# Layer-1 attention: the values' transpose moved to a slot's head, the output product moved to the next batch

## The reference

```python
qkv = x @ qkv_w.T + qkv_b                       # 16 heads of 8
scores = einsum('bhid,bhjd->bhij', q, k) / sqrt(8)
scores = scores + _alibi_bias(16, 256, 0.5)     # -|i - j| * slope[h]
attn = softmax(scores)
out = einsum('bhij,bhjd->bhid', attn, v)
x = x + (out @ out_w.T + out_b)
```

## Time and profile before

| what | value |
|---|---|
| median of 3 runs | 1610.66 us (1606.85 to 1613.25) |
| the profiled execution's own time | 1614.27 us |
| its span | 1612.5 us |
| mean granted TensorE clock over the span | 0.962 of full |
| TensorE busy over the span | 1464.5 us (91%) |
| VectorE busy over the span | 1071.1 us (66%) |
| ScalarE busy over the span | 1007.6 us (62%) |
| layer-1 attention's slots | about 950 to 1340 us of the span |

### The profile page before, as it was taken

How to read it: one execution, slowest core, us unless ns; L and a number is a source line. 1 busy time by engine, 2 the same in 40 slices (tenths; PEclk the granted TensorE clock), 3 DMA queues, 4 the chain that set the end, 5 groups by cost and what they waited for, 6 DMA issues and landing times. The chain is left out here.

```text
span 1612.5 us, 39525 instructions
## 1 busy us (share of the span) xinstructions
PE 1464.5 (91%) x11702; PEld 1106.8 (69%) x11703; DVE 1071.1 (66%) x3467; ACT 1007.6 (62%) x2671; POOL 503.1 (31%) x861
## 2 busy tenths in 40 slices
PE   7999999999999877889999878888888886999998
PEld 5777777777777644578888745555555554777697
DVE  6776777767777466656666537778777763775565
ACT  6887887878878446246666546666666663554454
POOL 4332333323333236033333131322223103552133
PEclk9999999999999987889999979999999997998999
DMA  6000000000000031011111110000000000000000
GB/s 212 2 0 0 0 0 0 0 0 0 0 0 1 25 152 33 27 30 42 46 42 42 33 52 9 13 13 7 13 13 11 8 2 0 2 1 1 1 27 26
DMA packets 34077, 35.77 MB, mean 22 GB/s; under 512 B 5472, under 2 KB 29664, under 8 KB 33120
## 3 DMA queue, kind: packets, MB, share of 16 engines
q1 hardware_dynamic: 29664, 26.08, 5.0%
q0 software_dynamic: 4352, 8.92, 2.2%
HBM read 26.07 MB, written 8.91 MB: 22 GB/s over the span
## 5 line engine op out<-in xcount | busy, mean ns | idle before, releaser
L671 POOL TENSOR_SCALAR a_prob<-a_prob,a_inv 128x128 f32<-128x128 f32 (+1 forms) x256 | 126.4, 504 | 336.5 <-DVE a_inv L547 336.5
L474 ACT ACTIVATE a_prob<-a_psS,a_low 128x128 f32<-128x128 f32 (+1 forms) x512 | 208.8, 427 | 0.9 <-DVE a_low L537 0.9
L537 DVE CUSTOM_DVE_ANT_0 a_psS<-a_psS,a_bias 128x128 f32<-128x128 f32 (+1 forms) x512 | 167.5, 388 | 42.8 <-PE a_psS L322 38.6
L1831 ACT ACTIVATE a_probT<-a_psZ 128x512 f32<-128x512 f32 x256 | 139.1, 595 | 89.3 <-PE a_psZ L1617 70.7
L1914 DVE TENSOR_REDUCE a_low<-a_psS 128x4 f32<-128x1024 f32 x128 | 156.2, 1220 | 52.9 <-remote 34.6
L465 ACT COPY a_probT<-a_psT 128x384 f32<-128x384 f32 x256 | 122.6, 479 | 77.7 <-PE a_psT L368 69.1
L368 PE MATMUL a_psT<-ident,a_prob 128*128 128x128 f32 x768 | 132.8, 282 | 3.7 <-ACT a_probT L465 1.8
L1357 POOL DMA_INDIRECT d_rows<-rows_dram,source x72 | 68.2, 947 | 187.2 <-PE e_psX L1440 134.7
L322 PE MATMUL a_psS<-a_qk 64*128 64x128 f32 (+1 forms) x1024 | 120.0, 353 | 3.2 <-issue 1.4
L368 PEld LDWEIGHTS a_psT<-ident,a_prob 128*128 128x128 f32 x768 | 84.7, 140 | 45.4 <-issue 34.3
L358 PE MATMUL a_psO<-a_probT,a_v 128*64 128x256 f32 (+1 forms) x1024 | 111.5, 339 | 0.0
(11 more groups left out here) (376 smaller groups left out, 4159.2 us busy)
## 6 DMA issues: line engine op xcount, KB each, us to landing
sorted_out<-e_y SPq DMA_DIRECT2D x72, 64.0 KB, 1.5
in_lo<-in_gate_up SPq DMA_DIRECT2D x4, 1024.0 KB, 7.9
x<-in_x SPq DMA_DIRECT2D x8, 256.0 KB, 6.8
down<-in_down SPq DMA_DIRECT2D x1, 2048.0 KB, 16.5
rows_dram<-rows SPq DMA_DIRECT2D x8, 256.0 KB, 2.2
out<-x SPq DMA_DIRECT2D x8, 256.0 KB, 2.3
d_rows<-rows_dram,source POOLq DMA_INDIRECT x72
cw<-in_count_wide SPq DMA_DIRECT2D x1, 1024.0 KB, 4.7
```

The costliest lines, as they stand in the source:

```text
L474: nc.scalar.activation(prob[:, 2 * (p % 4) + k, lo:hi], psS[:, u, lo:hi], ACT.Exp, bias=low[:, u, i:i + 1], scale=-1.0, accum_out=total[:, ...
L537: nc.vector.tensor_tensor_reduce(psS[:, u, lo:hi], psS[:, u, lo:hi], bias0[:, 2 * p + k, lo:hi], 1.0, LEAST, ALU.add, ALU.min, low[:, u, i ...
L671: nc.gpsimd.tensor_scalar(w, w, inv[:, 2 * (q % 2) + 1, i:i + 1], 1.0, ALU.mult, ALU.mult).then_inc(norm_done[1], 1)
L1831: nc.scalar.activation(probT[:, (p + half + 1) % 2, 2 * half + c, :, :].rearrange("p j s -> p (j s)"), psZ[:, c, :], ACT.Exp, scale=-1.0). ...
```

## The change

1. `turn_values` moves from between the first and the second scores to the head of the next slot, ahead of `turn_lows`. It then needs no wait for `shift` of the same slot, but for that of the slot before. `oT` gets two buffers, as the unit's result now lies one slot longer. `divide` handles the unit that is four slots old (p - 4) instead of three, and `turn_lows` no longer waits for `o_norm`.
2. The transpose of `o_rows` (`turn_rows`) and the copy to `o_cols` move from slot 2 to slot 3, ahead of `values`.
3. The product with `wo1` (`output`) moves from the end of slot 2 to the head of slot 0 of the next batch.
4. `choice_kept` and `out_statistics` move from slot 3, where they stand on either side of `lows(b, 3, 1)`, to slot 0 of the next batch, where both stand between `divide` and `lows(b, 0, 1)`.
5. `ln.apply`, `ln.turn` and `ln.keep` move from slot 0 to slot 1. On VectorE `ln.apply` stands there between `divide` and `statistics`.

```diff
--- before.py
+++ after.py
@@ -1546,7 +1546,7 @@
         low = ph.sb("low", [P, 2, BT, P])
         probT = ph.sb("probT", [P, 2, 4, BT, S])
         v_aug = ph.sb("v_aug", [P, BT, H, VW])
-        oT = ph.sb("oT", [P, S])
+        oT = ph.sb("oT", [P, 2, S])
         inv = ph.sb("inv", [P, BT, 4])
         o_rows = ph.sb("o_rows", [P, BT, D])
         o_cols = ph.sb("o_cols", [P, S])
@@ -1684,23 +1684,39 @@
                 pe.wait_ge(low_done, n * 2)
                 if not (isinstance(b, int) and b == 0 and p == 1):
                     pe.wait_ge(qm4_done, n - 1)
-                if not (isinstance(b, int) and b == 0):
-                    pe.wait_ge(o_norm, n - 3)
                 for i in range(BT):
                     mm = pe.transpose(psT[:, i * P:(i + 1) * P], low[:, (p + 1) % 2, i, :], g.ident[:])
                 mm.then_inc(lowt_done, 1)
 
-            def turn_values(b, p, lagging):
+            def turn_values(b, p, new):
 
                 n = b * 4 + p
-                pe.wait_ge(o_kept, n - 2)
-                if lagging:
-                    pe.wait_ge(qm4_done, n)
+                pe.wait_ge(o_kept, n - 3)
+                if new or p < 2:
+                    pe.wait_ge(qm4_done, n - 1)
+                if not (isinstance(b, int) and b == 1 and p == 0):
+                    pe.wait_ge(o_norm, n - 4)
+                for i in range(BT):
+                    mm = pe.transpose(psT[:, S + i * P:S + (i + 1) * P], oT[:, p % 2, i * P:(i + 1) * P], g.ident[:])
+                mm.then_inc(ot_done, 1)
+
+            def turn_rows(b, prep):
+
+                pe.wait_ge(o_norm, b * 4)
+                if prep:
+                    pe.wait_ge(cur_ready, b + 2)
                 else:
-                    pe.wait_ge(o_norm, n - 3)
+                    ln.wait_kept(pe, b - 1)
                 for i in range(BT):
-                    mm = pe.transpose(psT[:, S + i * P:S + (i + 1) * P], oT[:, i * P:(i + 1) * P], g.ident[:])
-                mm.then_inc(ot_done, 1)
+                    mm = pe.transpose(psM[:, i * P:(i + 1) * P], o_rows[:, i, :], g.ident[:])
+                mm.then_inc(oc_done, 1)
+
+            def output(count):
+
+                pe.wait_ge(oc_kept, count)
+                for i in range(BT):
+                    mm = pe.matmul(psM[:, i * P:(i + 1) * P], o_cols[:, i * P:(i + 1) * P], g.wo1[:], start=True, stop=True)
+                mm.then_inc(y_done, 1)
 
             def context_keys():
 
@@ -1740,12 +1756,14 @@
                 for p in range(4):
                     old, older = has_unit(p, 4), has_unit(0, 8)
                     n = b * 4 + p
+                    if p == 0 and older:
+                        output(b - 1)
+                    if old:
+                        turn_values(b, p, new)
                     if has_unit(p, 1):
                         turn_lows(b, p)
                     if new or has_unit(p, 2):
                         first_scores(b, p, new, has_unit(p, 2))
-                    if has_unit(p, 3):
-                        turn_values(b, p, has_unit(p, 1))
                     if new and p < 3:
                         if p == 2:
                             pe.wait_ge(v_kept, b + 1)
@@ -1762,16 +1780,8 @@
                         ln_in.turn(pe, b + 1, psM)
                     if new or has_unit(p, 1):
                         second_scores(b, p, new, has_unit(p, 1))
-                    if p == 2 and old:
-
-                        pe.wait_ge(o_norm, b * 4)
-                        if prep:
-                            pe.wait_ge(cur_ready, b + 2)
-                        else:
-                            ln.wait_kept(pe, b - 1)
-                        for i in range(BT):
-                            mm = pe.transpose(psM[:, i * P:(i + 1) * P], o_rows[:, i, :], g.ident[:])
-                        mm.then_inc(oc_done, 1)
+                    if p == 3 and old:
+                        turn_rows(b, prep)
                     if has_unit(p, 2):
                         values(b, p)
                     if new and p == 1:
@@ -1782,15 +1792,11 @@
                     if prep and p == 2:
                         pe.wait_ge(qk4_kept, n + 2)
                         project(b + 1)
-                    if p == 2 and old:
-                        pe.wait_ge(oc_kept, b)
-                        for i in range(BT):
-                            mm = pe.matmul(psM[:, i * P:(i + 1) * P], o_cols[:, i * P:(i + 1) * P], g.wo1[:], start=True, stop=True)
-                        mm.then_inc(y_done, 1)
-                    if p == 0 and older:
+                    if p == 1 and older:
                         pe.wait_ge(y_used, b - 1)
                         ln.turn(pe, b - 2, psM)
                     if p == 3 and not new:
+                        output(b)
                         pe.wait_ge(y_used, b)
                         ln.turn(pe, b - 1, psM)
 
@@ -1863,17 +1869,17 @@
                         keep_in(b + 1)
                     if has_unit(p, 1):
                         exps(b, p, 0)
-                    if p == 2 and old:
+                    if p == 3 and old:
                         act.wait_ge(oc_done, b)
                         nc.scalar.copy(o_cols[:], psM[:, 0:S]).then_inc(oc_kept, 1)
                     if has_unit(p, 2):
                         act.wait_ge(pv_done, n - 1)
-                        if not (isinstance(b, int) and b == 0 and p == 2):
-                            act.wait_ge(ot_done, n - 2)
-                        nc.scalar.copy(oT[:], psO[:, 0:S]).then_inc(o_kept, 1)
+                        if old:
+                            act.wait_ge(ot_done, n - 3)
+                        nc.scalar.copy(oT[:, p % 2, :], psO[:, 0:S]).then_inc(o_kept, 1)
                     if prep and p == 2:
                         keep_qk(b + 1)
-                    if p == 0 and older:
+                    if p == 1 and older:
                         ln.keep(act, b - 2, psM[:, 0:S], act_seen)
                     if p == 3 and not new:
                         ln.keep(act, b - 1, psM[:, 0:S], act_seen)
@@ -1923,14 +1929,13 @@
                 v.tensor_tensor(qm4[:, (p + 1) % 2, :], psT[:, 0:S], qk4[:, G, 0, :].bitcast(F32), ALU.add).then_inc(qm4_done, 1)
 
             def divide(b, p):
-                m = b * 4 + p - 3
-                G = (p + 1) % 4
+                m, G = b * 4 + p - 4, p
                 dve.wait_ge(ot_done, m + 1)
                 rows = psT[:, S:2 * S].rearrange("p (i h c) -> p i h c", i=BT, c=VW)
                 v.reciprocal(inv[:], rows[:, :, :, DH1]).then_inc(inv_done, 1)
                 dve.wait_ge(inv_done, m + 1)
-                if p == 3 and not (isinstance(b, int) and b == 0):
-                    dve.wait_ge(oc_done, b)
+                if p == 0 and not (isinstance(b, int) and b == 1):
+                    dve.wait_ge(oc_done, b - 1)
                 for i in range(BT):
                     x = v.tensor_tensor(o_rows[:, i, 4 * G * DH1:4 * (G + 1) * DH1].rearrange("p (h c) -> p h c", h=4),
                                         rows[:, i, :, 0:DH1], inv[:, i, :].unsqueeze(2).to_broadcast([P, 4, DH1]), ALU.mult)
@@ -1983,14 +1988,15 @@
                         split_lo(b + 1)
                     if new:
                         lows(b, p, 0)
-                    if has_unit(p, 3):
+                    if old:
                         divide(b, p)
                     if p == 0 and older:
+                        choice_kept(b - 1)
+                        out_statistics(b - 1)
+                    if p == 1 and older:
                         ln.apply(dve, b - 2)
                     if prep and p == 1:
                         statistics(b + 1)
-                    if p == 3 and old:
-                        choice_kept(b)
                     if new:
                         lows(b, p, 1)
                     if prep and p == 0:
@@ -1998,9 +2004,9 @@
                         add_choice(b + 1, 1)
                     if prep and p == 1:
                         ln_in.apply(dve, b + 1)
-                    if p == 3 and old:
+                    if p == 3 and not new:
+                        choice_kept(b)
                         out_statistics(b)
-                    if p == 3 and not new:
                         ln.apply(dve, b - 1)
 
             rounds_of_four(dve, first, slots)
```

## The result

The changed kernel took 1638.94 us (median of 4 runs, 1637.33 to 1642.62), the kernel before beside it 1611.95: a ratio of 1.0172, 95% interval 1.0142 to 1.0203. It is 1.7% slower. Its profiled execution took 1639.7 us with a span of 1637.9, against 1614.27 and 1612.5.

A forecast was written before the change was run, and what follows sets the result against it. The prediction took the ring of VectorE reductions through psS, not TensorE's busy share, as the bound. Terms -0.25 + 1.0 + 0.7 + 0.62 gave +2.07 us a batch, +28 overall: 1638 against the median, range 1618 to 1648.

The forecast's parts named there:

- a ring of reductions: Eight VectorE reductions per batch: scores await the reduction ahead to free psS, the next reduction awaits scores; legs total 23.56 us.
- Slot 2: Two legs between reduction starts, 8.03 us together; forecast gain 0.25 us a batch from ScalarE losing o_cols, bounds 0 and 1.35.
- The head: Slot 3's second leg, 2.80 us, into slot 0's head: TensorE's longer queue ahead of turn_lows adds 1.0 us, bounds 0.91 to 1.29.
- Slot 0's first leg: Leg of 2.33 us: VectorE loses ln.apply, gains choice_kept and out_statistics; forecast +0.7 us, bounds 0.6 and 0.8.
- Slot 1's first leg: Leg of 2.37 us, full on VectorE: ln.apply comes on top; forecast +0.62 us, bounds 0.55 and 0.64.
- The batch: One batch of the loop, slot 2 to slot 2: forecast +2.07 us, 25.6 instead of 23.56.
- The drain: The draining tail at the kernel's end: called the same serial chain, with no added time forecast.
- Rival 1: Slot 2: the hold goes with TensorE's removed wait, gaining 1.35 us a batch; 14 us less than forecast, 1624; chance 0.22.
- the hold: Slot 2, first leg: TensorE's completions reach other engines late while gathers are under way, 1.10 us a batch; forecast to stay.
- rival 2: Every slot: faster, as TensorE bounds them, its two waits vanish and nothing on VectorE shows; 11 us less, 1600; chance 0.11.
- rival 3: No change: the hold goes and slot 0's extra VectorE work is covered; 0.3 us a batch, 1614; chance 0.11.
- rival 4: More than forecast: the head costs 1.29 us, slot 0 0.8, and slot 2's ScalarE chain gains nothing; 1647; chance 0.04.

The follow-up runs named there:

- e3: Changed kernel with the edits of e1 and e2, and the output product between the first and second scores of slot 0; 1589.9 us, ratio 0.998.
- b_before: The kernel before, unchanged, traced again in the second group, on a chip without the hold; 1587.93 us in one run.
- a_after: The changed kernel once more, without the hold, against the kernel before; 1618.05 us against 1593.07, ratio 1.0148.
- e8: e3 with layer-norm transposes between slot 1's scores, and slot 2's query/key projection and scaling put first; without the hold 1578.3 us, ratio 0.990.
- e9: Changed kernel with one line moved: output product between the first and second scores of slot 0 instead of at its head; ratio 1.0081.
- e1: Changed kernel with part 1 undone: values' transpose back between the scores, one oT, o_rows' transpose beside it in slot 3; 1613.92 us, ratio 1.0133.
- e2: Changed kernel with layer-norm statistics moved to slot 2, application to slot 3's end, its transpose and copy to the next batch's slot 1; ratio 1.0063.
- b2_before: The kernel before, unchanged, traced again in the third group, on a chip with the hold; 1623.6 us in one run.
- e10: The kernel before without the gathers of batches 2 to 15, on a chip with the hold; 1592.62 us against 1616.95, ratio 0.9856.
- e6: The kernel before with the gathers issued in slot 0 of the next batch, one batch further ahead, on a chip without the hold; ratio 1.0003.
- e11: The same kernel as e8, run again on a chip with the hold; 1628.9 us against 1616.95 for the kernel before, ratio 1.0075.
- e4: The kernel before without the gathers of batches 2 to 15, on a chip without the hold; ratio 0.9976.

## Why the prediction was right

The direction, the time (1638 forecast, 1638.94 measured) and the kind of cause were right; that the total came within 1 us was luck.

- **Reading the batch as a ring of reductions** held in every kernel. TensorE's 90% busy share was no bound: e3 puts 0.55 us of product into a leg of 2.33 and the leg stays.
- **Slot 2** was sized right: -0.25 forecast, -0.27 measured. The 0.85 us stop of TensorE that the change removes was worth nothing by itself, as the leg ends on ScalarE's chain and `split_lo`: from `b_before` to `a_after`, where there was no such stop to remove, the leg still gains 0.23. e8 shows it from the other side: starting that chain earlier takes 1 us off.
- **The head** was forecast at +1.0 and came at +0.55. The term had TensorE's pairs of transposes at 0.37 each and let the new work fill only part of the idle 0.38. The rows after show 0.31 and 0.21 for the pairs (1121.84 to 1122.15, 1123.78 to 1123.99); the first begins ahead of the reduction, so that `values` starts only 0.22 behind it. And the new work filled all of the idle time. The loop's turn was in it: where batch 14 goes over into batch 15, which is written out, the kernel before has a head leg of 2.63 instead of 2.80. In the changed kernel this leg is 3.34, against 3.35 in the loop, and `values` and the product lie 1.08 apart, so the turn costs nothing while TensorE has work issued. 0.22 + 0.55 + 0.21 - 0.38 is 0.60. e9 and e1 show the parts: the pairs without the product add nothing, the product without the pairs 0.33.
- **Slot 0's first leg** was forecast at +0.7 and came at +0.96. The pieces are as sized, but the waits of VectorE on its own results, which I had put at 0.1 together, show as idle 0.15 before the statistics and 0.25 before their aggregation, and `divide` takes some 0.1 longer (0.67, 1126.42 to 1127.09). e2 takes the whole term away; of slot 0 it moves only the statistics.
- **Slot 1's first leg**: +0.62 forecast, +0.50 measured. The 0.64 was read from a row whose end was a wait for scores; back to back the pair of applications takes 0.51 (1133.00 to 1133.51). What the forecast didn't see is that VectorE isn't alone there: TensorE's queue in slot 1, two pairs longer, asks for the same time. With VectorE's piece gone (e2) slot 1 still takes 5.61 us, as in the changed kernel, against 5.17 before. The sentence that `ln.turn` and `turn_values` are hidden in slot 1 holds only while VectorE is late.
- **The batch**: +2.07 forecast, +1.69 measured; 22.4 us from the first reduction to the last in place of 28.6.
- **The drain**: "the same serial chain" is what failed. It took 3.9 us more, and the traces let this be parted. From the last reduction to the last application, with the full clock through all three groups of `values`, the kernel before takes 14.6 us (1323.05 to 1337.65) and the changed one 16.2 (`a_after`, 1328.69 to 1344.88). So 1.6 is the change's: 0.8 from the longer queue ahead of the last `turn_lows` (2.12 us behind the reduction's start instead of 1.29), and 0.8 behind the last `values`, where the chain now has another turn of the values ahead of the transpose of `o_rows` (3.41 instead of 2.62 us). The other 2.3 go with the clock, and that isn't the change's alone: `b_before` took 16.1 us with one group of `values` at 1.93 us, `b2_before` 18.0 with two. What decides which execution gets it isn't shown. The batches were forecast 6 us too dear and the drain 4 too cheap, and the kernel before took 1.3 us more in this pair than the median that the sum began with. That these three nearly cancel made the total right. TensorE's rows of `a_after` in the drain, to be set beside 1349.79 and 1354.05 above:

```profile
1333.86 1.07 PE L1677 MATMUL a_psO<-a_probT,a_v_aug 128*32 128x256 f32 x16
...
1337.13 1.07 PE L1677 MATMUL a_psO<-a_probT,a_v_aug 128*32 128x256 f32 x16 [1.06 <-ACT a_probT L1837]
```

- **Rival 1** (the hold goes with TensorE's stop) is refuted. With the stop gone the hold stayed (first leg 4.39, slot 2's pair 7.81 where 7.8 was forecast), taking the gathers away on such a chip removes it (e10), and the stop itself comes only with the hold (the rows of `b_before`). The page that I had weighed, the Trainium skill, SBUF — State Buffer, section "Who interferes with whom", says that PE and ACT never wait on anyone. The starts of TensorE's matmuls are in keeping with that, 2.03 us behind the reduction in either kind. But the reduction that waits for them starts late beside gathers on some chips, 4.45 us after the one before it against 2.33 in e10's pair, and for the kernel this comes to the same. That the gathers can't make the hold, which I had weighed as following from that sentence, is refuted by e10; there the measurement decides. What the way is by which gathers do this, and what differs between the chips, stays open; e6 was to show whether the hold follows the gathers to another slot and met a chip without it.
- **Rivals 2, 3 and 4** did not come: slot 0's leg did grow, against rivals 2 and 3. Of rival 4, slot 0's leg went beyond its 0.8 and the head stayed far below its 1.29.

## What to carry to other kernels

Where a single buffer makes a ring between two engines, cost a moved piece by the leg that it enters, not by the engine's busy share: 0.55 us of TensorE was free between two scores and cost 0.55 us at a slot's head. A stop that a change removes is worth only what the next chain in line lets through, here nothing of 0.85 (the 0.27 that slot 2 gained is ScalarE's copy); and a queue that looks hidden may be hidden by the cost that you are about to remove. Check a version on more than one chip before calling it better: the kernel of e8 and e11 is 1.0% faster on one and 0.75% slower on another.

## What the runs showed of the hardware

The same program has a batch of 22.46 us on one chip and 23.56 or 23.67 on others. The whole difference lies in slot 2, beside four indirect gathers, though GpSimd's issue of them and the starts of TensorE's matmuls are timed alike on both. With the gathers gone the two kinds agree (22.43 in e4's trace, 22.42 in e10's). In e11's trace TensorE's clock falls to 1.2 GHz behind stops of 1.4 us in seven batches of eleven; hold and clock together cost up to 5.4 us a batch (26.8 in e11's slowest batch of the loop, 21.4 in e8's). A fall for a part of one batch came without the hold as well: in e1's batch of 1159.02 the granted clock over slot 1's first leg was 0.54, and the leg took 3.67 us instead of 2.87.
